# Attention stage: four of a quad's 32 row maxima are taken by ScalarE and GpSimd

## The chip, the cores and the metric

The kernel runs on one core of a Trainium2 chip. The metric is device time in microseconds (us), the median of several runs. Before the change it is 6462.87 us (three runs, 6459.95 to 6463.46). The engines are TensorE (PE in the profile; its weight loads are PEld), VectorE (DVE), ScalarE (ACT), GpSimd (POOL), and SyncE (SP), which issues the DMAs.

## The reference

Sixteen batches of 1024 tokens with 256 features go through differential attention with 16 heads (each with two score maps of head dimension 8), then through an expert layer in which each of 32 experts picks 8 tokens. Only the attention core is touched by the change:

```python
q = rope(q).transpose(0, 2, 1, 3) * scaling
k = rope(k).transpose(0, 2, 1, 3)
scores = jnp.einsum('bhqd,bhkd->bhqk', q, k)
probs = jax.nn.softmax(scores.astype(jnp.float32), axis=-1)
w = probs[:, :, 0] - lam * probs[:, :, 1]
attn = jnp.einsum('bhqk,bhkd->bhqd', w, v)
```

The softmax needs the maximum of each score row of 1024 keys before the exponentials are taken.

## The kernel before

The program has stages that follow each other: `project`, `attend`, `route`, `experts`, `scatter`. The change is in `attend` (L448), which runs from about 593 us to about 5816 us of the span. There are 512 score maps, handled in 128 *quads* of four. For each quad two things are computed:

- *Trials* (`attempt`, L769): for quad n+1, 32 tiles of 128 queries x 1024 keys. Each is two matmuls into one of two PSUM buffers `ps_m` (`j % 2`), and `maximum` (L662) on VectorE reduces it to the row maximum in `largest`. The first matmul of trial j waits (L774) until trial j-2 has been reduced.
- *Scores* (`score`, L740): for quad n, 64 transposed tiles of 128 keys x 512 queries, into one of three PSUM slots `ps_e`. ScalarE takes their exponentials (L650). The row maximum is already subtracted, since three extra rows of `q_stack` hold it, split into three bf16 parts. Score j waits (L747) for the exponential of score j-3.

`weighted_sums` (L753) multiplies the exponentials, with the values, into `ps_o`. A quad has 16 *periods* g. In each, TensorE issues in order: score 0 and half of trial 2g, score 1 and the other half, the weighted sums of two periods ago, score 2 and half of trial 2g+1, score 3 and the other half (`period`, L782). VectorE's order is `period` at L687: maximum 2g, then the transposes due in this period, then maximum 2g+1. The transposes are:

- g = 0: `turn_maxima` of the second side (c = 1, trials 16 to 31); g = 8: that of the next quad's first side (c = 0, trials 0 to 15);
- g = 1 and g = 9: `turn_sums`; g = 2: `invert`; g = 7: `turn_out`.

After `turn_maxima`, GpSimd runs `split` (L577: five small instructions), then SyncE runs `load_rows` (L522): it stores the parts to memory with four DMAs, waits until they have landed, and loads them into the extra rows of `q_stack` with one more DMA. TensorE waits for these rows (`rows_loaded`, L787) ahead of score 0 of period 0 (first side) and of period 8 (second side). GpSimd also runs `finish` (L591), which ends the quad before. SyncE's order in a quad is `turn` (L545): rows of side 0, values, rows of side 1, then `load_stacks` (18 DMAs, 1.5 MB, for the quad four ahead, once the last score of the present quad is done), then `store`.

Below, the *mark* of a period is the start of ScalarE's exponential of its score 2. In the traces a row of four exponentials begins at each mark.

Of the kernel before, what the change touches and what calls it, by code (L numbers as in the profile page):

```python
# [45 lines left out]
EPS = 1e-5  # L46
THETA = 0.0001
# [30 lines left out]
class Build:  # L78
# [369 lines left out]
    def attend(self):  # L448
# [22 lines left out]
        loops = quads // BUFS - 1  # L471
        with ExitStack() as ctx:
# [10 lines left out]
            zeros, negated, rest = sb("zeros", [P, BLK]), sb("negated", [P, BLK]), sb("rest", [P, BLK])  # L483
# [25 lines left out]
            out_stored, pool_step = [sem("out_stored0"), sem("out_stored1")], sem("pool_step")  # L509
            ONES = 5  # L510
            SPLIT_STEPS, FINISH_STEPS = 4, 10
# [3 lines left out]
            def _(sp):  # L515
# [53 lines left out]
            def _(pool):  # L569
# [7 lines left out]
                def split(h, base):  # L577

                    pool.wait_ge(max_turned, h + 1)
                    nc.gpsimd.tensor_tensor(negated[:], zeros[:], largest_t[:], ALU.subtract).then_inc(pool_step, 1)  # L580
                    if not (isinstance(h, int) and h == 0):
                        pool.wait_ge(max_stored, 16 * (P // BLK) * h)
                    nc.gpsimd.tensor_tensor(parts[:, 0], zeros[:], largest_t[:], ALU.subtract).then_inc(pool_step, 1)
                    pool.wait_ge(pool_step, base + 2)
                    nc.gpsimd.tensor_tensor(rest[:], negated[:], parts[:, 0], ALU.subtract).then_inc(pool_step, 1)
                    pool.wait_ge(pool_step, base + 3)
                    nc.gpsimd.tensor_tensor(parts[:, 1], rest[:], zeros[:], ALU.add).then_inc(pool_step, 1)
                    pool.wait_ge(pool_step, base + 4)
                    nc.gpsimd.tensor_tensor(parts[:, 2], rest[:], parts[:, 1], ALU.subtract).then_inc(split_done, 1)

# [29 lines left out]
                def turn(n, rows, base):  # L620
                    if rows:
                        for c in range(2):
                            split(2 * (n + AHEAD) + c, base)
                            base = base + SPLIT_STEPS
                    finish(n, base)

                for h in range(2 * AHEAD):
                    split(h, SPLIT_STEPS * h)
                pool.wait_ge(lam_done, 1)
                start, steps = 2 * AHEAD * SPLIT_STEPS, 2 * SPLIT_STEPS + FINISH_STEPS  # L630
                with hinted(nc, pool, 0, loops) as i:
                    for u in range(BUFS):
                        turn(BUFS * i + u, True, start + steps * (BUFS * i + u))
                for u in range(BUFS):
                    n = BUFS * loops + u
                    turn(n, u < BUFS - AHEAD, start + steps * n - 2 * SPLIT_STEPS * max(0, u - (BUFS - AHEAD)))

            @block.scalar
            def _(act):
                act.wait_ge(lam_dots, 1)  # L640
                nc.scalar.activation(lam_exp[:], lam_dot[:], ACT.Exp).then_inc(lam_exps, 1)
                act.sem_inc(exp_done, SLOTS)
                with hinted(nc, act, 0, loops + 1) as i:
                    for u in range(BUFS):
                        n = BUFS * i + u
                        for j in range(HALVES):
                            act.wait_ge(scores_done, HALVES * n + j + 1)
                            if j % QUAD == 0:
                                act.wait_ge(sums_done, GROUPS * n + j // QUAD + 1 - E_GROUPS + E_GROUPS)
                            nc.scalar.activation(e[:, j % E_BUFS], ps_e[:, (HALVES * u + j) % SLOTS], ACT.Exp,  # L650
                                                 scale=SCALE).then_inc(exp_done, 1)

            @block.vector
            def _(dve):
# [7 lines left out]
                def maximum(m, u, j):  # L662
                    dve.wait_ge(tries_done, TRIES * m + j + 1)
                    nc.vector.reduce_max(largest[:, u % 2, j // SIDE, j % SIDE:j % SIDE + 1], ps_m[:, j % 2], AX.X).then_inc(max_done, 1)  # L664

                def turn_maxima(m, u, c):

                    dve.wait_ge(max_done, TRIES * m + SIDE * (c + 1) + 2)
# [18 lines left out]
                def period(n, u, g, tries, rows=True, last_quad=True, this_quad=True):  # L687
                    if tries:
                        maximum(n + AHEAD, u + AHEAD, 2 * g)
                    if g == 0 and rows:  # L690
                        turn_maxima(n, u, 1)
                    if g == TILES and rows:
                        turn_maxima(n + 1, u + 1, 0)
# [41 lines left out]
            def _(pe):  # L735
# [33 lines left out]
                def attempt(m, u, j, half):  # L769
# [3 lines left out]
                    if half == 0:  # L773
                        pe.wait_ge(max_done, TRIES * m + j + 1)  # L774
# [777 lines left out]
```

## Time and profile before

| | before |
|---|---|
| median of three runs | 6462.87 us |
| the profiled execution | 6450.77 us (span 6449.0 us) |
| PE busy | 5794.4 us (90%) |
| DVE busy | 5879.4 us (91%) |
| ACT busy | 4718.1 us (73%) |
| POOL busy | 1947.2 us (30%) |
| granted TensorE clock, mean | 0.96; 0.99 to 1.00 in most of `attend` |
| row maxima, L664 | 4096 of 1211 ns each |
| exponentials, L650 | 8192 of 602 ns each |

The busy shares are means over the whole program. In the middle of `attend` the windows show more: between 3000 and 4000 us VectorE is busy for 978 us, TensorE for 953, ScalarE for 824 and GpSimd for 247. Instructions of one engine overlap at their ends, so that a group's time on the engine is read from the spacing of its starts and not from the mean duration. A row of the timeline merges consecutive instructions of one group; `x4` is their number, and the bracket says how long the engine stood idle ahead of the row and who ended that.

### The profile page before, as it was taken

To read this page: it belongs to the slowest core of one execution; us is meant where nothing else is said; L and a number is where in the kernel's file an instruction comes from. 1 tells how busy PE (TensorE), PEld (TensorE's weight loads), DVE (VectorE), ACT (ScalarE), POOL (GpSimd) and SP (SyncE) were. 2 spreads that over 40 slices of the span, in tenths; PEclk is the share of its full clock that TensorE was granted. 3 is DMA by queue.
4 is the path that set the end of the run, shared out by engine and by line. 5 is a ranking of instruction groups with operands and counts; after the bars stand their busy time and mean duration, and the time that the engine had idled before them with its cause. 6 is when DMAs were issued, how large, how long until landed. Compare 5 with 4: busy or idle time off the path is not lost. (4 is left out here: it accounts for less than half of the span.)

```text
span 6449.0 us, 136849 instructions
## 1 busy us (share of the span) xinstructions
PE 5794.4 (90%) x36560; PEld 1816.8 (28%) x36560; DVE 5879.4 (91%) x6456; ACT 4718.1 (73%) x8950; POOL 1947.2 (30%) x3270
## 2 busy tenths in 40 slices
PE   7776999999999999999999999999999999997775
PEld 4442222222222222222222222222222222224423
DVE  7998999999999999999999999999999999986716
ACT  4553878888788888887888888888878888783304
POOL 6774222222222222222222222222222222225506
PEclk8886999999999999999999999999999999998878
DMA  4554222222222222222222222222222222205688
GB/s 145 152 160 121 40 46 48 48 48 50 46 48 48 48 48 48 48 48 48 48 48 48 48 48 48 48 48 48 48 48 48 48 48 48 47 19 179 197 314 282
DMA packets 435720, 491.57 MB, mean 76 GB/s; under 512 B 106451, under 2 KB 288883, under 8 KB 435171
## 3 DMA queue, kind: packets, MB, share of 16 engines
q1 hardware_dynamic: 434147, 483.60, 31.2%
q8 instruction: 359, 5.88, 0.4%
q14 instruction: 190, 1.56, 0.1%
q10 hardware_dynamic: 1024, 0.53, 0.0%
HBM read 360.60 MB, written 123.21 MB: 75 GB/s over the span
## 5 line engine op out<-in xcount | busy, mean ns | idle before, releaser
L650 ACT ACTIVATE at_e<-at_ps_e 128x512 f32<-128x512 f32 x8192 | 4236.1, 602 | 944.1 <-PE at_ps_e L748 943.9
L664 DVE TENSOR_REDUCE at_largest<-at_ps_m 128x1 f32<-128x1024 f32 x4096 | 4777.2, 1211 | 156.4 <-PE at_ps_m L775 95.9
L775 PE MATMUL at_ps_m<-k_stack,q_stack 48*128 48x512 bf16 x8192 | 2725.2, 387 | 159.7 <-DVE at_largest L664 112.3
L748 PE MATMUL at_ps_e<-q_stack,k_stack 51*128 51x512 bf16 x8192 | 2478.6, 383 | 154.3 <-ACT at_e L650 69.1
L763 PE MATMUL at_ps_o<-at_e,at_v 128*32 128x512 f32 x16384 | 2255.2, 623 | 0.1
L748 PEld LDWEIGHTS at_ps_e<-q_stack,k_stack 51*128 51x128 bf16 x8192 | 624.5, 94 | 2520.6 <-ACT at_e L650 2216.6
L580 POOL TENSOR_TENSOR at_negated<-at_zeros,at_largest_t 128x32 f32<-128x32 f32 x256 | 64.8, 253 | 3244.3 <-DVE at_largest_t L671 3244.3
L775 PEld LDWEIGHTS at_ps_m<-k_stack,q_stack 48*128 48x128 bf16 x8192 | 620.1, 93 | 924.0 <-DVE at_largest L664 884.9
L763 PEld LDWEIGHTS at_ps_o<-at_e,at_v 128*32 128x32 f32 x16384 | 450.3, 149 | 525.5 <-issue 340.3
L615 POOL TENSOR_TENSOR at_rms<-at_mean_eps,at_minus_half 128x16 f32<-128x16 f32 x128 | 372.7, 2912 | 10.0
L429 PE MATMUL pr_ps_q<-pr_xn_t,pr_w 128*128 128x512 f32 x512 | 232.8, 597 | 1.5 <-issue 0.8
L676 DVE STREAM_TRANSPOSE at_sums_t<-at_ps_o 128x512 f32<-128x512 f32 x256 | 180.3, 704 | 28.8 <-PE at_ps_o L763 28.6
L312 ACT CAST pr_parts<-pr_rotated 128x1024 bf16<-128x1024 f32 x64 | 66.7, 1043 | 177.4 <-DVE pr_rotated L373 177.4
L271 POOL TENSOR_TENSOR pr_swapped<-pr_swapped,pr_sin 128x1024 f32<-128x1024 f32 x64 | 164.5, 2571 | 97.7 <-DVE pr_swapped L387 97.7
L595 POOL TENSOR_TENSOR at_inverse<-at_inverse,at_neg_lam 128x16 f32<-128x16 f32 x128 | 27.8, 217 | 539.5 <-DVE at_inverse L680 539.5
L263 POOL TENSOR_TENSOR pr_parts<-pr_rest,pr_parts 128x1024 bf16<-128x1024 f32 x64 | 182.4, 2851 | 11.8 <-ACT pr_parts L316 11.8
L1016 ACT ACTIVATE ro_x<-ro_ps_y,ro_y_bias,ro_y_rstd 128x256 f32<-128x256 f32 x128 | 61.9, 564 | 163.7 <-POOL ro_y_bias L978 163.7
L417 PE MATMUL pr_ps_t<-ident,pr_xn 128*128 128x128 f32 x256 | 59.6, 410 | 125.6 <-ACT pr_xn L298 72.7
L609 POOL TENSOR_TENSOR at_square<-at_square 128x128 f32<-128x128 f32 (+3 forms) x512 | 158.5, 309 | 40.1
L379 DVE TENSOR_TENSOR pr_rest<-pr_rotated,pr_parts 128x1024 f32<-128x1024 f32 x64 | 168.6, 2635 | 0.0
L439 PE MATMUL pr_ps_v<-pr_w,pr_xn_t 128*128 128x256 f32 x512 | 159.4, 468 | 2.4 <-ACT pr_v_out L331 2.4
L373 DVE TENSOR_TENSOR pr_rotated<-pr_by_cos,pr_swapped 128x1024 f32<-128x1024 f32 x64 | 143.1, 2236 | 9.3 <-issue 9.3
(128 smaller groups left out, 3082.2 us busy)
## 6 DMA issues: line engine op xcount, KB each, us to landing
k_stack<-k_parts SPq DMA_DIRECT2D x1536, 64.0 KB
q_stack<-q_parts SPq DMA_DIRECT2D x256, 192.0 KB
q_stack<-q_parts SPq DMA_DIRECT2D x256, 128.0 KB
w_first<-in_w SPq DMA_DIRECT2D x32, 1024.0 KB, 11.7
ex_w_second<-in_w SPq DMA_DIRECT2D x32, 1024.0 KB, 12.7
q_parts<-pr_parts SPq DMA_DIRECT2D x96, 256.0 KB, 2.9
k_parts<-pr_parts SPq DMA_DIRECT2D x96, 256.0 KB, 2.9
pr_x_in<-in_x SPq DMA_DIRECT2D x16, 1024.0 KB, 6.2
```

What stands on the lines that cost most here:

```text
L263: nc.gpsimd.tensor_tensor(parts[:, ch, 2], rest[:, ch % 2], parts[:, ch, 1], ALU.subtract).then_inc(part3_done, 1)
L271: nc.gpsimd.tensor_tensor(swapped[:, ch % 2], swapped[:, ch % 2], sin[:], ALU.mult).then_inc(sin_done, 1)
L379: nc.vector.tensor_tensor(rest[:, ch % 2], rotated[:, ch % 2], parts[:, ch, 0], ALU.subtract).then_inc(rest_done, 1)
L429: last = nc.tensor.matmul(ps_q[:, ch % 2, half * HALF:(half + 1) * HALF], w[:, k, ch // KC, cols], xn_t[:, u, k, half * HALF:(half + 1) * ...
L439: last = nc.tensor.matmul(ps_v[:, ch % 2, j * D:(j + 1) * D], xn_t[:, u, k, t * P:(t + 1) * P], w[:, k, 2, :], start=(k == 0), stop=(k == ...
L615: nc.gpsimd.tensor_tensor(rms[:], mean_eps[:], minus_half[:], ALU.pow).then_inc(pool_step, 1)
L650: nc.scalar.activation(e[:, j % E_BUFS], ps_e[:, (HALVES * u + j) % SLOTS], ACT.Exp, scale=SCALE).then_inc(exp_done, 1)
L664: nc.vector.reduce_max(largest[:, u % 2, j // SIDE, j % SIDE:j % SIDE + 1], ps_m[:, j % 2], AX.X).then_inc(max_done, 1)
L676: nc.vector.transpose(sums_t[:, c].rearrange("p b d -> p (b d)"), ps_o[:]).then_inc(sums_read, 1)
L748: nc.tensor.matmul(ps_e[:, (HALVES * u + j) % SLOTS], k_stack[rows, u, pair, c, kt * P:(kt + 1) * P], q_stack[rows, u, pair, c, half * HAL ...
L763: last = nc.tensor.matmul(ps_o[32 * tile:32 * tile + 32, :], v[:, u, tile // 2, kt::TILES], e[:, (QUAD * g + tile) % E_BUFS], start=(kt == ...
L775: last = nc.tensor.matmul(ps_m[:, j % 2, half * HALF:(half + 1) * HALF], q_stack[rows, u, pair, c, t * P:(t + 1) * P], k_stack[rows, u, pa ...
```

## The change

- VectorE no longer reduces trials 5, 15, 19 and 25 of a quad (`FOLDED`), each the second trial of its period: of the periods 2, 7, 9 and 12. ScalarE copies such a trial (128x1024) from PSUM to `fold_in` after the fourth exponential of that period. GpSimd folds the copy twice (1024 to 512 to 256). A fold is a maximum built of three instructions: subtract, clamp at zero, add. VectorE then reduces two folded trials in one instruction (2 x 256), inside `turn_maxima`.
- `turn_maxima` moves from periods 0 and 8 to periods 2 (side 1) and 12 (side 0). It now waits for the folds.
- The maxima are reduced with a sign change, and `split` loses one of its five instructions.
- GpSimd's order per quad becomes: split of side 1, finish, folds 0 and 1, split of side 0, folds 2 and 3.
- SyncE issues `load_stacks` ahead of the rows of side 1.
- TensorE's trial two behind a folded one waits for ScalarE's copy.

```diff
+        FOLDED = (5, 15, 19, 25)
+        REDUCED = TRIES - FOLDS
+        TURNS = (TILES + 4, 2)
...
                     if rows:
                         load_rows(n + AHEAD, (u + AHEAD) % BUFS, 0)
                         load_v(n + AHEAD, (u + AHEAD) % BUFS)
-                        load_rows(n + AHEAD, (u + AHEAD) % BUFS, 1)
                     if load:
                         sp.wait_ge(scores_done, HALVES * (n + 1))
                         load_stacks(n + BUFS, u)
+                    if rows:
+                        load_rows(n + AHEAD, (u + AHEAD) % BUFS, 1)
                     store(n, u)
...
+                def fold(m, k, base):
+                    c, x = k // 2, fold_in[:, k % 2]
+                    pool.wait_ge(copied, FOLDS * m + k + 1)
+                    for width in (S // 2, S // 4):
+                        low, high = x[:, 0:width], x[:, width:2 * width]
+                        nc.gpsimd.tensor_tensor(high, high, low, ALU.subtract).then_inc(pool_step, 1)
+                        pool.wait_ge(pool_step, base + 1)
+                        pool.sem_inc(passed, 1)
+                        nc.gpsimd.tensor_scalar(high, high, LARGEST, 0.0, ALU.min, ALU.max).then_inc(pool_step, 1)
+                        pool.wait_ge(pool_step, base + 2)
+                        if width > WIDTH:
+                            nc.gpsimd.tensor_tensor(low, low, high, ALU.add).then_inc(pool_step, 1)
+                            pool.wait_ge(pool_step, base + 3)
+                            base = base + 3
+                        else:
+                            if not (isinstance(m, int) and m == 0):
+                                pool.wait_ge(folds_read, 2 * m + c - 1)
+                            nc.gpsimd.tensor_tensor(fold_out[:, c, k % 2], low, high, ALU.add).then_inc(fold_done, 1)
...
+                def turn(n, this, following, base):
+                    if this:
+                        split(2 * n + 1, base)
+                        base = base + SPLIT_STEPS
+                    finish(n - 1, base)
+                    base = base + FINISH_STEPS
+                    if following:
+                        base = folds(n + AHEAD, (0, 1), base)
+                        split(2 * (n + AHEAD), base)
+                        folds(n + AHEAD, (2, 3), base + SPLIT_STEPS)
...
+                def copy_trial(m, k):
+                    act.wait_ge(tries_done, TRIES * m + FOLDED[k] + 1)
+                    if not (isinstance(m, int) and m == 0 and k < 2):
+                        act.wait_ge(fold_done, FOLDS * m + k - 1)
+                    nc.scalar.copy(fold_in[:, k % 2], ps_m[:, FOLDED[k] % 2]).then_inc(copied, 1)
...
+                        if tries and j % QUAD == QUAD - 1 and j // 2 in FOLDED:
+                            copy_trial(n + AHEAD, FOLDED.index(j // 2))
...
                 def turn_maxima(m, u, c):
-                    dve.wait_ge(max_done, TRIES * m + SIDE * (c + 1) + 2)
+                    dve.wait_ge(fold_done, FOLDS * m + 2 * (c + 1))
+                    first, second = FOLDED[2 * c] % SIDE, FOLDED[2 * c + 1] % SIDE
+                    columns = slice(first, second + 1, second - first)
+                    nc.vector.tensor_reduce(largest[:, u % 2, c, columns], fold_out[:, c], AX.X, ALU.max,
+                                            negate=True).then_inc(folds_read, 1)
+                    dve.wait_ge(folds_read, 2 * m + c + 1)
+                    dve.wait_ge(max_done, REDUCED * m + REDUCED // 2 * (c + 1) + 2)
...
-                    if half == 0:
-                        pe.wait_ge(max_done, TRIES * m + j + 1)
+                    if half == 0 and j - 2 in FOLDED:
+                        pe.wait_ge(copied, FOLDS * m + FOLDED.index(j - 2) + 1)
+                    elif half == 0:
+                        pe.wait_ge(max_done, REDUCED * m + (reduced_before(j - 1) if j else -1) + 2)
```

## Rows read from the trace of the kernel before

**Rows 1.** The page's group of the exponentials, line 650.

```profile
L650 ACT ACTIVATE at_e<-at_ps_e 128x512 f32<-128x512 f32 x8192 | 4236.1, 602 | 944.1 <-PE at_ps_e L748 943.9
```

**Rows 2.** The tile at_e: duration min/median/max in ns, first and last start.

```profile
L650 ACT ACTIVATE at_e<-at_ps_e x8192: 590/598/653, 634.3 to 5813.3; 128x512 f32<-128x512 f32 x200
```

**Rows 3.** Timeline (start us, us), ACT, periods 2 to 4, 8 to 11 of one quad.

```profile
3112.62 2.07 ACT L650 ACTIVATE at_e<-at_ps_e 128x512 f32<-128x512 f32 x4 [0.36 <-PE at_ps_e L748]
3115.28 2.06 ACT L650 ACTIVATE at_e<-at_ps_e 128x512 f32<-128x512 f32 x4 [0.59 <-PE at_ps_e L748]
3117.74 2.06 ACT L650 ACTIVATE at_e<-at_ps_e 128x512 f32<-128x512 f32 x4 [0.40 <-PE at_ps_e L748]
...
3127.43 2.06 ACT L650 ACTIVATE at_e<-at_ps_e 128x512 f32<-128x512 f32 x4 [0.36 <-PE at_ps_e L748]
3130.09 2.07 ACT L650 ACTIVATE at_e<-at_ps_e 128x512 f32<-128x512 f32 x4 [0.59 <-PE at_ps_e L748]
3132.53 2.07 ACT L650 ACTIVATE at_e<-at_ps_e 128x512 f32<-128x512 f32 x4 [0.37 <-PE at_ps_e L748]
3135.30 2.06 ACT L650 ACTIVATE at_e<-at_ps_e 128x512 f32<-128x512 f32 x4 [0.71 <-PE at_ps_e L748]
```

**Rows 4.** Timeline, ACT, periods 10 and 11 of the quad before that.

```profile
3092.98 2.06 ACT L650 ACTIVATE at_e<-at_ps_e 128x512 f32<-128x512 f32 x4 [0.36 <-PE at_ps_e L748]
3095.64 2.06 ACT L650 ACTIVATE at_e<-at_ps_e 128x512 f32<-128x512 f32 x4 [0.60 <-PE at_ps_e L748]
```

**Rows 5.** Timeline, PE, one regular period from score 0 to the next score 2.

```profile
3061.79 0.38 PE L748 MATMUL at_ps_e<-q_stack,k_stack 51*128 51x512 bf16 x1
...
3062.42 0.39 PE L748 MATMUL at_ps_e<-q_stack,k_stack 51*128 51x512 bf16 x1
...
3062.74 1.09 PE L763 MATMUL at_ps_o<-at_e,at_v 128*32 128x512 f32 x8
3063.77 0.39 PE L748 MATMUL at_ps_e<-q_stack,k_stack 51*128 51x512 bf16 x1
```

**Rows 6.** Timeline, DVE: ten maxima back to back, then a transpose.

```profile
3073.06 11.78 DVE L664 TENSOR_REDUCE at_largest<-at_ps_m 128x1 f32<-128x1024 f32 x10
3084.76 0.70 DVE L685 STREAM_TRANSPOSE at_out<-at_attn_t 128x512 f32<-128x512 f32 x1
```

**Rows 7.** Groups by line and shape, ACT: instructions on 1024 elements.

```profile
L1262 ACT ACTIVATE ex_hidden<-ex_ps_h 128x1024 f32<-128x1024 f32 x8 | 8.2, 1024 | 65.3 <-PE ex_ps_h L1305 65.3
L316 ACT CAST pr_parts<-pr_rest 128x1024 bf16<-128x1024 f32 x64 | 66.9, 1045 | 82.1 <-DVE pr_rest L379 80.5
```

**Rows 8.** Groups by line and shape, POOL.

```profile
L271 POOL TENSOR_TENSOR pr_swapped<-pr_swapped,pr_sin 128x1024 f32<-128x1024 f32 x64 | 164.5, 2571 | 97.7 <-DVE pr_swapped L387 97.7
L598 POOL TENSOR_TENSOR at_normed<-at_sums_t,at_inverse 128x512 f32<-128x512 f32 x128 | 135.5, 1058 | 10.0
L604 POOL TENSOR_TENSOR at_square<-at_attn 128x256 f32<-128x256 f32 x128 | 78.6, 614 | 10.0
L580 POOL TENSOR_TENSOR at_negated<-at_zeros,at_largest_t 128x32 f32<-128x32 f32 x256 | 64.8, 253 | 3244.3 <-DVE at_largest_t L671 3244.3
L1249 POOL COPY ex_tokens<-merged_t 128x256 f32 x8 | 3.2, 400 | 150.4 <-PE ex_ps_o L1322 117.1 <-PEq L1286 33.3
```

**Rows 9.** Timeline, SP: stacks issued first, then rows of side 0, then of side 1.

```profile
3114.08 1.16 SPq L59 DMA_DIRECT2D q_stack<-q_parts  x3
...
3129.86 1.83 SPq L528 DMA_DIRECT2D max_parts<-at_parts  x4
3135.66 0.78 SPq L531 DMA_DIRECT2D q_stack<-max_parts  x1
...
3149.41 1.83 SPq L528 DMA_DIRECT2D max_parts<-at_parts  x4
3152.26 0.78 SPq L531 DMA_DIRECT2D q_stack<-max_parts  x1
```

**Rows 10.** DMA issues by line: count, KB each, median us to landing.

```profile
at_v<-v_tiles SPq DMA_DIRECT2D x128, 128.0 KB, 2.2
```

More of the change, by code:

```diff
@@ L46 @@
 EPS = 1e-5
+LARGEST = float(np.finfo(np.float32).max)
 THETA = 0.0001
@@ L471, in attend, with reduced_before @@
         loops = quads // BUFS - 1
+        FOLDED = (5, 15, 19, 25)
+        FOLDS = len(FOLDED)
+        WIDTH = S // 4
+        REDUCED = TRIES - FOLDS
+        TURNS = (TILES + 4, 2)
+        def reduced_before(j):
+            return sum(i not in FOLDED for i in range(j))
         with ExitStack() as ctx:
@@ L618, in finish, with folds @@
                                             ALU.mult).then_inc(attn_done, 1)
[L620 to L628, printed above, removed]
+                def folds(m, ks, base):
+                    for k in ks:
+                        fold(m, k, base)
+                        base = base + FOLD_STEPS
+                    return base
@@ L629, in _ @@
+                for c in range(2):
+                    base = folds(0, (2 * c, 2 * c + 1), base)
+                    split(c, base)
+                    base += SPLIT_STEPS
+                base = folds(1, (0, 1), base)
+                split(2, base)
+                base = folds(1, (2, 3), base + SPLIT_STEPS)
                 pool.wait_ge(lam_done, 1)
-                start, steps = 2 * AHEAD * SPLIT_STEPS, 2 * SPLIT_STEPS + FINISH_STEPS
+                steps = 2 * SPLIT_STEPS + FINISH_STEPS + FOLDS * FOLD_STEPS
@@ L631, in _ @@
                 with hinted(nc, pool, 0, loops) as i:
                     for u in range(BUFS):
[L633 to L636, printed above, removed]
+                        turn(BUFS * i + u + 1, True, True, base + steps * (BUFS * i + u))
+                base += steps * BUFS * loops
@@ new lines, in turn @@
+                def turn(n, u, tries):
+                    for j in range(HALVES):
+                        act.wait_ge(scores_done, HALVES * n + j + 1)
+                        if j % QUAD == 0:
+                            act.wait_ge(sums_done, GROUPS * n + j // QUAD + 1 - E_GROUPS + E_GROUPS)
+                        nc.scalar.activation(e[:, j % E_BUFS], ps_e[:, (HALVES * u + j) % SLOTS], ACT.Exp,
+                                             scale=SCALE).then_inc(exp_done, 1)
+                        if tries and j % QUAD == QUAD - 1 and j // 2 in FOLDED:
+                            copy_trial(n + AHEAD, FOLDED.index(j // 2))
@@ L640, in _ @@
+                for k in range(FOLDS):
+                    copy_trial(0, k)
                 act.wait_ge(lam_dots, 1)
                 nc.scalar.activation(lam_exp[:], lam_dot[:], ACT.Exp).then_inc(lam_exps, 1)
-                act.sem_inc(exp_done, SLOTS)
-                with hinted(nc, act, 0, loops + 1) as i:
+                with hinted(nc, act, 0, loops) as i:
                     for u in range(BUFS):
[L645 to L651, printed above, removed]
+                        turn(BUFS * i + u, u, True)
@@ L653, in _ @@
+                for u in range(BUFS):
+                    turn(BUFS * loops + u, u, u < BUFS - AHEAD)
             @block.vector
@@ L689, in period @@
                         maximum(n + AHEAD, u + AHEAD, 2 * g)
-                    if g == 0 and rows:
+                    if g == TURNS[1] and rows:
                         turn_maxima(n, u, 1)
-                    if g == TILES and rows:
+                    if g == TURNS[0] and tries:
                         turn_maxima(n + 1, u + 1, 0)
```

27 lines of the change are left out of this document (18 added, 9 removed).

## The prediction, made before the changed kernel was run

> **What bounds the kernel now.** I read the page first. It shows VectorE and TensorE about equally busy over the program, so the shares do not say which of them sets the pace. I then read the attention stage period by period. The 8192 exponentials run from 634.3 to 5813.3 us [rows 2], which is 5179.0/128 = 40.46 us a quad. The timeline of ScalarE gives the length of each period as the distance of two marks. A regular period takes 2.42 us, and sixteen of these are 38.8. In the quad of [rows 3] five periods are longer: 2 to 3 takes 2.66, 3 to 4 takes 2.46, 8 to 9 2.66, 9 to 10 2.44 and 10 to 11 2.77, together 0.89 us above 5 x 2.42. The quads that follow the loop's back edge, one in four, have 0.24 there in their second half in place of 0.61 [rows 4]. The mean extra is 0.80 us a quad. The rest of the 40.46, some 0.9, is waiting at the loop edges, which the change leaves alone.
>
> What sets the 2.42? TensorE's rows show it [rows 5]: score 1 (3062.42) waits for the exponential that began at the mark 3061.77, since that frees its slot (0.65 after the mark). The weighted sums follow at +0.32, the next score 2 at +1.03 more (3063.77), and its exponential starts 0.42 later, the next mark. 0.65 + 0.32 + 1.03 + 0.42 = 2.42. This is a ring of TensorE and ScalarE, with no VectorE in it. VectorE needs 11.70/10 = 1.17 us per maximum [rows 6], so 2.34 in a regular period, and 0.63 more where it transposes 512 columns. It falls behind in the periods with transposes and regains 0.08 a period. What it is late by shows up as the 0.80. So **VectorE costs the ring 0.80 us a quad, and nothing can be gained from relieving it beyond that**, although it is busy nearly all the time.
>
> How much room has ScalarE in the ring? Four exponentials span 2.06 with a last duration of 0.60 [rows 1, 3], so they start 0.487 apart. Four take 1.95, and 0.47 of the period's 2.42 is free.
>
> **The change part by part.** All sums are for 127 quads, those in which trials run beside scores, against the profiled execution of 6450.8 us. The median of the runs shown is 12.1 above it.
>
> *Removed: the lateness of VectorE.* Four of 32 maxima go, 4 x 1.17 = 4.7 us a quad. Two reductions of 2 x 256 elements come back; by the transpose of 512 columns they take 0.63 each. In periods 2, 7, 9 and 12 VectorE now has 1.17 + at most 1.1 us, within 2.42. Period 1 keeps two maxima and a transpose, 0.55 us over, but before the change it was followed by a delay only when period 0's and 2's small work was added. I take the whole 0.80 as gone: -0.80 x 127 = **-102 us**; bounds -102 and -60 (period 1 keeps a third).
>
> *Added: the copy on ScalarE.* Before is no copy of 1024 elements out of PSUM. The nearest row is the activation of 1024 from PSUM, 1024 ns; a cast of 1024 in SBUF has 1045 [rows 7]. Instructions of ScalarE overlap by 0.602 - 0.487 = 0.115, so the copy takes 0.91 to 0.93 of the engine; I take 0.92. It stands behind the exponential of score 3, with those of the next scores 0 and 1 and then score 2, the next mark, behind it. That mark comes at 4 x 0.487 + 0.92 = 2.87 after its own, not 2.42. The 0.47 free in the period is used up and 0.44 to 0.45 is left over. It is not regained: the following score 1 waits for the delayed exponential, and the ring starts anew from there with its 2.42. So 4 x 0.44 x 127 = **+224 us**. Bounds: 0.42 if the overlap is as large as seen (213), 0.57 if the copy has no overlap at either end (290).
>
> The Trainium skill gives another price for this copy (ScalarE: Activation LUTs, What ACT_TABLE_LOAD costs): 186 ns plus 0.833 ns an element, with an overlap of 93 between neighbours. It would be 0.946 us here and 237 us in place of 224; the exponentials' 602 stand beside its 612. The same page prices a change of the table set at 2.7 us, which would be ruinous with copies among exponentials; in this trace copies and exponentials share the routing stage without such a load.
>
> *Added: folds on GpSimd.* Four instructions with two inputs and two with one, per trial. At 512 elements a two-input instruction takes 1.06, half of the 1024-element row's 2.57 would be 1.29; at 256 it takes 0.61 [rows 8]. For the clamp the lower bound is the copy, 0.40 at 256 and some 0.63 at 512; for the upper bound I take twice a two-input instruction. With 0.08 between dependent ones a trial takes 4.8 to 7.9 us; I take 5.4 (clamp near the copy's row, since it has one input). Cover: side 1 is the tighter. Its two folds run after the split of side 0 (about 2.3 after the mark of period 12) and must end at VectorE's turn in period 2 of the next quad, 13.7 us later. So 6.8 us a trial is free, and at 5.4 this costs **0**. ScalarE's copy also waits for the fold two before; that is done 2.9 us ahead.
>
> The Trainium skill advises elementwise work on VectorE, since GpSimd is about half as fast with two inputs (GPSIMD Engine Reference, 4.1 Engine selection). Its 2.6 cycles an element at 1.2 GHz are 1.11 us for 512; the row's 1.06 agrees. By it the move costs GpSimd some 22 us a quad, which the idle engine has.
>
> *Moved: the turn of side 0, from period 8 to 12.* From turn to landed rows it takes: split 4 x 0.33 (0.25 each, [rows 8], and a gap), issue and landing of the parts 2.85, from 3149.41 to 3152.26 [rows 9], then 2.2 as for the values [rows 10], some 6.6 in all. The turn ends its reduce near 0.95 behind the mark, so the rows land at +7.6. TensorE needs them ahead of score 0 of the next quad, which is issued at the mark of period 15: 3 x 2.42 + 0.44 = +7.7, and may slip by 0.4 more before score 1 is late. Half a microsecond of cover; single quads will miss it: **+5 us**, bounds 0 and +40.
>
> *Moved: SyncE's 18 stack loads ahead of the rows of side 1.* Here the trace has a warning. In the quad of [rows 9] the parts of side 0 were issued at 3129.86, 15.8 us after the stacks (3114.08), and the next step came only 5.80 us later, not 2.85: parts queue behind stacks still under way, until some 20 us after their first issue. In other quads the stacks are through after 13 to 17. Now the parts of side 1 always queue behind them. The stacks start 2.4 us ahead of the quad's first mark, so the rows land 13 to 21 us after it; they are needed by 7 x 2.42 + 0.44 + 0.4 = 17.8. A quarter of the quads is late by a microsecond or so: **+38 us**, bounds 0 and +115.
>
> *Start and end.* Before the first quad VectorE waits for the folds of trials 15 and 25, less the four maxima: **+3 us**. The final quad is as before.
>
> Sum: -102 + 224 + 0 + 5 + 38 + 3 = +168. 6450.8 + 168 = 6619, and 12 for the median: **6630 us**.
>
> **Rivals.** *The copies are covered (faster).* If the copy's 0.92 found room in the ring, as it would if the three `ps_e` slots let ScalarE work ahead, only the -102 would be left: 6361 us. For it speaks that ScalarE is busy for 73% only. Against it: its idle time comes in pieces of 0.36 to 0.47 once a period [rows 3], and the slots are refilled only as fast as it empties them. It decides if the exponential behind the copy starts the next mark before 2.42 + 0.20, for then 4 x 0.20 equals the 0.80. Chance 0.09.
>
> *A draw.* Half of a copy's excess is hidden and the rows come in time: 6440 to 6475 us. Chance 0.03.
>
> *The folds become the bound (slower still).* From 6.8 us a trial on, each 0.1 more costs 0.2 us a quad, because VectorE stands in `turn_maxima` with all later maxima behind it, and TensorE behind those. At 7.6 it is 1.6 x 127 = 203, so 6833 us. The clamp is the one instruction with no row. Chance 0.08.
>
> *The rows of side 1 are late in most quads.* Stacks and parts then take 20 us each time, as in [rows 9]: 3 us a quad for most, some 250 us, 6840 us. Chance 0.04.
>
> The forecast itself (the copies exposed, the folds hidden) has 0.76; its own range is 6560 to 6720.
>
> **How the numbers follow.** Low end: copies 213, lateness -102, no late rows, and 60 us less waiting at loop edges if the stack loads' new place frees the instruction fetches: 6514; I take 6530. High end: copies 290, lateness -60, rows 40 and 115: 6849 for all at once; I take 6750, which leaves out most of the two slow rivals. A measurement of this kernel can tell 0.2%, 13 us, from no change. Faster 0.09, same 0.03, slower 0.88.
>
> **What would show it.** Right: ScalarE's marks 2.42 apart except after periods 2, 7, 9 and 12, with 2.85 to 2.9 there; no idle of ScalarE in these four; the longer periods of [rows 3] gone; VectorE idle some 4 us a quad more; the copy near 1.02 us; a fold's six instructions within 6.8 us. Late rows would show as a wait of TensorE ahead of score 0 of period 8. Wrong: periods with a copy at 2.42 (first rival), or VectorE idle ahead of the 2 x 256 reduction (third).

## The result and the profile after

The changed kernel takes 6669.86 us (median of four runs, 6632.57 to 6688.60) against 6461.99 us before: a ratio of 1.0315, with a 95% interval from 1.0270 to 1.0359. It is slower by 208 us. The profiled execution took 6688.60 us against 6450.77, 238 us more; the sums below are made against that. Two later comparisons of the same kernel gave 1.0441 and 1.0408 (6744.66 and 6713.44 us). What varied is told with the experiments.

The page of the changed kernel, with busy time and share:

```profile
span 6686.8 us, 145310 instructions
PE 5835.6 (87%) x36560; PEld 1835.6 (27%) x36560; DVE 5534.0 (83%) x6200; ACT 5146.6 (77%) x9462; POOL 4426.4 (66%) x6086
L704 ACT ACTIVATE at_e<-at_ps_e 128x512 f32<-128x512 f32 x8192 | 4258.2, 618 | 751.6 <-PE at_ps_e L822 750.2
L697 ACT COPY at_fold_in<-at_ps_m 128x1024 f32<-128x1024 f32 x512 | 522.4, 1020 | 43.1 <-PE at_ps_m L851 43.1
```

VectorE really has been relieved: 5534 us where it had 5879, and between 3000 and 4000 us of the span 864 us where it had 978. The program is longer all the same. The tile at_e gives the length of the attention stage, as [rows 2] did (durations in ns, then first and last start):

```profile
L704 ACT ACTIVATE at_e<-at_ps_e x8192: 588/606/686, 638.4 to 6050.2; 128x512 f32<-128x512 f32 x200
```

5411.8/128 = 42.28 us a quad where [rows 2] gave 40.46. That is 1.82 more, and the stage starts 4 us later; together this is all of the 238.

Where in the quad? ScalarE's timeline answers to [rows 3] (start, duration, idle before). The first exponential of a period is its mark. The rows show periods 2 to 7, then 9:

```profile
3273.62 1.08 ACT L704 ACTIVATE at_e<-at_ps_e 128x512 f32<-128x512 f32 x2 [0.36 <-PE at_ps_e L822]
3274.59 1.02 ACT L697 COPY at_fold_in<-at_ps_m 128x1024 f32<-128x1024 f32 x1
3275.48 3.08 ACT L704 ACTIVATE at_e<-at_ps_e 128x512 f32<-128x512 f32 x6
3278.92 2.06 ACT L704 ACTIVATE at_e<-at_ps_e 128x512 f32<-128x512 f32 x4 [0.36 <-PE at_ps_e L822]
3281.35 2.06 ACT L704 ACTIVATE at_e<-at_ps_e 128x512 f32<-128x512 f32 x4 [0.36 <-PE at_ps_e L822]
...
3286.20 1.08 ACT L704 ACTIVATE at_e<-at_ps_e 128x512 f32<-128x512 f32 x2 [0.36 <-PE at_ps_e L822]
...
3291.49 1.09 ACT L704 ACTIVATE at_e<-at_ps_e 128x512 f32<-128x512 f32 x2 [0.36 <-PE at_ps_e L822]
3292.47 1.02 ACT L697 COPY at_fold_in<-at_ps_m 128x1024 f32<-128x1024 f32 x1
3293.36 3.08 ACT L704 ACTIVATE at_e<-at_ps_e 128x512 f32<-128x512 f32 x6
3296.80 2.06 ACT L704 ACTIVATE at_e<-at_ps_e 128x512 f32<-128x512 f32 x4 [0.36 <-PE at_ps_e L822]
```

Two exponentials, the copy, then six exponentials without a gap: ScalarE has nothing free there. From the mark of period 2 (3273.62) to that of period 4 (3278.92) it is 5.30 us, where two regular periods take 4.85. One copy costs the ring 0.45 to 0.46 us. Periods 9 and 10 show the same, 3291.49 to 3296.80.

The mean length of each period in us, worked out from the starts of the exponentials of 122 quads (the third to the 124th):

```
period          0    1    2    3   4-6    7    8    9   10   11   12   13   14   15   quad
before        2.42 2.42 2.66 2.46 2.42 3.12 2.62 2.44 2.75 2.42 2.42 2.42 2.42 2.63  40.50
after         2.46 2.42 2.83 2.47 2.42 3.91 2.57 2.83 2.47 2.42 2.83 2.47 2.42 2.96  42.34
b_relief      2.43 2.42 2.66 2.42 2.42 3.24 2.49 2.42 2.42 2.42 2.42 2.42 2.42 2.63  40.11
a_nofold      2.44 2.43 2.83 2.47 2.42 3.69 2.58 2.83 2.47 2.43 2.83 2.47 2.43 2.95  42.12
a_copy2       2.43 2.42 3.73 2.48 2.42 3.93 2.66 3.73 2.60 2.47 3.74 2.59 2.49 2.63  45.17
a_sp          2.45 2.43 2.83 2.47 2.42 3.55 2.53 2.83 2.47 2.43 2.83 2.47 2.42 2.95  41.92
a_sp_turn11   2.42 2.42 2.83 2.47 2.42 3.63 2.53 2.83 2.48 2.43 2.94 2.43 2.42 2.63  41.74
half          2.42 2.45 2.45 2.42 2.42 2.78 2.66 2.43 2.45 2.42 2.45 2.42 2.42 2.63  39.69
b_sp          2.42 2.42 2.66 2.46 2.42 4.57 2.66 2.44 2.65 2.42 2.42 2.42 2.42 2.63  41.90
after_again   2.44 2.42 2.83 2.47 2.42 4.38 2.66 2.83 2.47 2.42 2.83 2.47 2.42 2.86  42.79
after_third   2.43 2.43 2.83 2.47 2.42 4.20 2.60 2.83 2.47 2.43 2.83 2.47 2.43 2.80  42.48
a_sp_again    2.44 2.43 2.83 2.47 2.42 3.52 2.54 2.83 2.49 2.43 2.83 2.47 2.43 2.88  41.87
```

The names are those of the experiments. Period 7 holds the wait at the loop's back edge in one quad of four, and period 15 a fixed 0.80 in another, before the change too.

Besides the copies two more places grew. In period 7 TensorE waits for the rows of side 1, which it needs ahead of score 0 of period 8. SyncE's timeline of a quad in which this happened (its first mark is at 3433.15, and it does not follow the back edge):

```profile
3431.11 1.13 SPq L60 DMA_DIRECT2D q_stack<-q_parts  x3
...
3435.93 2.13 SPq L66 DMA_DIRECT2D k_stack<-k_parts  x6
3441.17 1.87 SPq L541 DMA_DIRECT2D max_parts<-at_parts  x4
3451.06 0.78 SPq L544 DMA_DIRECT2D q_stack<-max_parts  x1
```

ScalarE's in its period 7:

```profile
3450.57 1.09 ACT L704 ACTIVATE at_e<-at_ps_e 128x512 f32<-128x512 f32 x2 [0.36 <-PE at_ps_e L822]
3451.54 1.02 ACT L697 COPY at_fold_in<-at_ps_m 128x1024 f32<-128x1024 f32 x1
3454.01 1.08 ACT L704 ACTIVATE at_e<-at_ps_e 128x512 f32<-128x512 f32 x2 [1.45 <-PE at_ps_e L822]
3456.51 2.06 ACT L704 ACTIVATE at_e<-at_ps_e 128x512 f32<-128x512 f32 x4 [1.42 <-PE at_ps_e L822]
```

and TensorE's, with score 0 of period 8 first:

```profile
3453.51 0.38 PE L822 MATMUL at_ps_e<-q_stack,k_stack 51*128 51x512 bf16 x1 [2.75 <-DMA q_stack<-max_parts]
...
3454.15 1.79 PE L837 MATMUL at_ps_o<-at_e,at_v 128*32 128x512 f32 x8
3455.87 0.61 PE L822 MATMUL at_ps_e<-q_stack,k_stack 51*128 51x512 bf16 x1
```

The parts were issued 10.1 us behind the first stack load, and the step after them came 9.89 us later and not 2.85 as in [rows 9] without stacks under way. The load of the rows (3451.06) then landed at 3453.39, and TensorE went on. The period took 5.94 us, 3.11 more than a copy explains. A part of that is TensorE itself, which ran at the lower of its two clock levels for a while behind the wait: the weighted sums took 1.79 us where [rows 5] has 1.09, and the granted clock was 0.65 in the mean between 3453.5 and 3456.5 us.

Over the 122 quads of the trace: the step from the issue of the parts of side 1 to the load of the rows took 6.5 us in the mean (2.9 to 11.1), where it was 3.0 before. The load itself took 2.3 to 2.5 us from issue to landing, every time and in both kernels. In 40 quads the rows landed after TensorE could have used them. None of the 40 is a quad behind the back edge: there the rows had landed by the mark of period 7 each time, so the wait at the back edge is for something else.

The view of waits puts 132.6 us of TensorE's idle time, in 115 waits, on the loads of the rows of both sides. About two thirds stand in period 7 (0.73 us a quad). The rest (0.33 a quad) stands in period 15, where TensorE waits for the rows of side 0, whose turn has moved to period 12.

### The profile page after: what moved, and what is told of

It reads as the page before. It is cut to its first block and busy times, and to the rows that moved or that the text cites. A ratio compares the mean times of both kernels' runs of the same rounds, so it can differ in the third digit from the quotient of the medians.

```text
span 6686.8 us, 145310 instructions
## 1 busy us (share of the span) xinstructions
PE 5835.6 (87%) x36560; PEld 1835.6 (27%) x36560; DVE 5534.0 (83%) x6200; ACT 5146.6 (77%) x9462; POOL 4426.4 (66%) x6086
## 3 DMA queue, kind: packets, MB, share of 16 engines
q14 instruction: 219, 1.79, 0.1%
q10 hardware_dynamic: 1024, 0.53, 0.0%
## 5 line engine op out<-in xcount | busy, mean ns | idle before, releaser
L731 DVE TENSOR_REDUCE at_largest<-at_ps_m 128x1 f32<-128x1024 f32 x3584 | 4237.5, 1217 | 679.8 <-PE at_ps_m L851 644.3
L822 PE MATMUL at_ps_e<-q_stack,k_stack 51*128 51x512 bf16 x8192 | 2648.0, 388 | 428.7 <-DMA q_stack<-max_parts 132.6
L851 PE MATMUL at_ps_m<-k_stack,q_stack 48*128 48x512 bf16 x8192 | 2812.3, 391 | 80.1 <-DVE at_largest L731 44.7
L837 PE MATMUL at_ps_o<-at_e,at_v 128*32 128x512 f32 x16384 | 2285.1, 630 | 0.1
L610 POOL TENSOR_TENSOR at_fold_in<-at_fold_in 128x512 f32<-128x512 f32 (+1 forms) x1024 | 1023.9, 1000 | 74.9 <-ACT at_fold_in L697 34.2
L596 POOL TENSOR_TENSOR at_parts<-at_largest_t,at_zeros 128x32 bf16<-128x32 f32 x256 | 64.3, 251 | 1147.4 <-DVE at_largest_t L745 1147.4
L616 POOL TENSOR_TENSOR at_fold_in<-at_fold_in 128x512 f32<-128x512 f32 x512 | 650.1, 1270 | 42.9
L613 POOL TENSOR_SCALAR at_fold_in<-at_fold_in 128x512 f32<-128x512 f32 (+1 forms) x1024 | 518.2, 506 | 202.8 <-POOL at_fold_in L610 199.9
L697 ACT COPY at_fold_in<-at_ps_m 128x1024 f32<-128x1024 f32 x512 | 522.4, 1020 | 43.1 <-PE at_ps_m L851 43.1
L622 POOL TENSOR_TENSOR at_fold_out<-at_fold_in 128x256 f32<-128x256 f32 x512 | 371.9, 726 | 53.5 <-POOL at_fold_in L613 21.1
```

The costliest lines, as they stand in the source:

```text
L610: nc.gpsimd.tensor_tensor(high, high, low, ALU.subtract).then_inc(pool_step, 1)
L613: nc.gpsimd.tensor_scalar(high, high, LARGEST, 0.0, ALU.min, ALU.max).then_inc(pool_step, 1)
L616: nc.gpsimd.tensor_tensor(low, low, high, ALU.add).then_inc(pool_step, 1)
L622: nc.gpsimd.tensor_tensor(fold_out[:, c, k % 2], low, high, ALU.add).then_inc(fold_done, 1)
L697: nc.scalar.copy(fold_in[:, k % 2], ps_m[:, FOLDED[k] % 2]).then_inc(copied, 1)
L731: nc.vector.tensor_reduce(largest[:, u % 2, j // SIDE, j % SIDE:j % SIDE + 1], ps_m[:, j % 2], AX.X, ALU.max, negate=True).then_inc(max_do ...
```

## The experiments

Times are medians beside the kernel before on the same chip; each such comparison gives a ratio.

**b_relief: the relief alone.** The kernel before, less four maxima:

```diff
+        LEFT_OUT = (5, 15, 19, 25)
                 def maximum(m, u, j):
+                    if j in LEFT_OUT:
+                        return
                     dve.wait_ge(tries_done, TRIES * m + j + 1)
```

> The kernel before, with the row maxima of trials 5, 15, 19 and 25 of each quad left out altogether (nobody reads these four trials) and nothing put in their place. It prices the relief of VectorE by itself. Theory (the ring of TensorE and ScalarE sets the period, VectorE's lateness costs 0.80 us a quad): 102 us less than before, 6360 us, and every period at 2.42 us. Rival (the busiest engine is the bound): 4 x 1.17 us a quad less, 594 us, 5870 us. Second rival (the five long periods have another cause than VectorE): no change, 6462 us.

Measured: 6403.67 us against 6453.13, ratio 0.9927 (0.9906 to 0.9947). So 49 us less, not 594: VectorE's busy share was no bound. The long periods 8, 9 and 10 are at 2.42 in three quads of four. The extra 0.24 in period 2 stays, as ScalarE's timeline shows:

```profile
3125.71 2.07 ACT L656 ACTIVATE at_e<-at_ps_e 128x512 f32<-128x512 f32 x4 [0.36 <-PE at_ps_e L756]
3128.37 2.06 ACT L656 ACTIVATE at_e<-at_ps_e 128x512 f32<-128x512 f32 x4 [0.59 <-PE at_ps_e L756]
3130.80 2.06 ACT L656 ACTIVATE at_e<-at_ps_e 128x512 f32<-128x512 f32 x4 [0.36 <-PE at_ps_e L756]
```

Period 1 still has two maxima and a transpose there. So of the 0.80 us a quad 0.56 went (71 us). Periods 7 and 8 of the quads behind the back edge took 8.44 us together, 7.79 before, which takes 0.16 a quad (20 us) back. The size expected for this run was too large, the mechanism was right.

**a_nofold: the folds made cheap.** Of each fold's three instructions only the last add stays.

> The changed kernel with the folds cut to their last add each (subtract and clamp are left out of both folds, so that the folded maxima are not maxima). GpSimd's work per trial falls from 5.65 us to about 2. Theory (the folds are hidden): within 20 us of the changed kernel, 6650 to 6690 us. Rival (the folds hold up VectorE's turn or slow its neighbours): 50 us less or more, 6620 us or below.

Measured: 6652.40 us, ratio 1.0323 (1.0288 to 1.0358), where the changed kernel had 1.0315. All periods but 7 and, slightly, 8, 0 and 15 are as in the changed kernel. Period 7 is 0.22 shorter; the total alone could not tell this from the changed kernel's own spread (6670 to 6745 us). VectorE's reduction of the folded trials settles it. In the changed kernel it waited for a fold only before the first quad:

```profile
L739 DVE TENSOR_REDUCE at_largest<-at_fold_out 128x2 f32<-128x512 f32 x256 | 172.4, 674 | 9.7 <-POOL at_fold_out L622 9.7
```

In the 122 quads the last fold had ended at least 1.75 us ahead of it. The folds cost nothing. GpSimd's groups in the changed kernel show what they take of GpSimd:

```profile
L610 POOL TENSOR_TENSOR at_fold_in<-at_fold_in 128x512 f32<-128x512 f32 x512 | 651.0, 1271 | 34.2 <-ACT at_fold_in L697 34.2
L613 POOL TENSOR_SCALAR at_fold_in<-at_fold_in 128x512 f32<-128x512 f32 x512 | 313.6, 613 | 102.9 <-POOL at_fold_in L610 100.0 <-issue 2.9
L610 POOL TENSOR_TENSOR at_fold_in<-at_fold_in 128x256 f32<-128x256 f32 x512 | 373.0, 728 | 40.7 <-POOL at_fold_in L616 0.7
L613 POOL TENSOR_SCALAR at_fold_in<-at_fold_in 128x256 f32<-128x256 f32 x512 | 204.6, 400 | 99.9 <-POOL at_fold_in L610 99.9
```

Two instructions of 1271, one of 613, two of 728 and one of 400 make 5.01 us; with the gaps a trial takes 5.65, inside the 6.8 that were free.

**a_copy2: the copy twice.**

```diff
+                    nc.scalar.copy(spare[:, k % 2], ps_m[:, FOLDED[k] % 2])
                     nc.scalar.copy(fold_in[:, k % 2], ps_m[:, FOLDED[k] % 2]).then_inc(copied, 1)
```

> The changed kernel with each trial copied twice by ScalarE, the first time into a tile that nobody reads. Theory (behind the first copy ScalarE has no room left in the ring): each further copy costs its full 0.91 us, 4 x 0.91 x 127 = 462 us more than the changed kernel's 6670, so 7130 us, unless part of it hides behind the wait for the rows of side 1 in period 7 (then 115 less, 7015). Rival (ScalarE, busy for 77%, takes copies in its idle time): less than 200 more, below 6870 us.

Measured: 7061.88 us, ratio 1.0952 (1.0928 to 1.0977): 392 more than the changed kernel's median, between the two numbers given. The timeline of ScalarE in period 2:

```profile
3399.02 1.08 ACT L706 ACTIVATE at_e<-at_ps_e 128x512 f32<-128x512 f32 x2 [0.36 <-PE at_ps_e L824]
3399.99 1.02 ACT L698 COPY at_spare<-at_ps_m 128x1024 f32<-128x1024 f32 x1
3400.89 1.04 ACT L699 COPY at_fold_in<-at_ps_m 128x1024 f32<-128x1024 f32 x1
3401.79 3.09 ACT L706 ACTIVATE at_e<-at_ps_e 128x512 f32<-128x512 f32 x6
3405.23 1.08 ACT L706 ACTIVATE at_e<-at_ps_e 128x512 f32<-128x512 f32 x2 [0.35 <-PE at_ps_e L824]
```

The copies start 0.90 apart, and periods 2, 9 and 12 are 3.73 where they were 2.83: every further copy costs its full 0.90. Periods 10 and 13, behind such copies, are 0.13 and 0.12 longer as well. In 17 and 18 of the 122 quads TensorE had the lower clock level there; period 10 took 3.31 us in these and 2.48 in the others. In period 7 the second copy was almost free (3.93 against 3.91), since the wait for the rows stood there anyway, and the wait in period 15 went, which fits the 0.9 us more that the rows of side 0 have from period 12 on.

**a_sp: SyncE's old order in the changed kernel.** The rows of side 1 are again issued ahead of the stack loads.

> The changed kernel with SyncE's old order: rows of side 1 first, the 18 stack loads behind them. Theory (in periods 7 to 8 the changed kernel waits for rows that queue behind the stacks, some 0.8 us a quad): 100 us less than the changed kernel, 6570 us, period 7 to 8 at 2.83 us except at the loop's back edge. Rival (that wait belongs to the later turn and split, or the queue is slow in any order): within 20 us of 6670.

Measured: 6630.02 us, ratio 1.0273 (1.0251 to 1.0296). Period 7 is 2.83 except at the back edge, as expected, and the total is 60 us above the number given. The gain beside the changed kernel's first measurement is only 40 us, because the waits at the back edge grew again: periods 7 and 8 of these quads took 8.45 us together, 6.87 in the changed kernel, 7.79 before. In the changed kernel the largest of 30 such pairs was 8.1 us; with the old order 8 of 30 took 10.8 to 13.7 (before the change 7 of 30 took 10.7 to 15.2).

**b_sp: that order in the kernel before.** One edit: stack loads ahead of the rows of side 1.

> The kernel before with one edit: SyncE issues the 18 stack loads ahead of the rows of side 1. Theory (the rows of side 1 then queue behind the stacks and reach period 8 late, whatever the turn; and the long waits at the loop's back edge are code that waits behind the same stacks and goes when these come earlier): period 7 to 8 longer by 0.8 to 1.5 us in three of four quads, no wait over 4 us at the back edge where the kernel before has 8 in 30; together 50 us more than before, 6500 us. Rival (the rows are late in the changed kernel because their turn moved from period 0 to 2): no change, 6450 us, period 7 to 8 at 2.42.

Measured: 6636.43 us against 6459.11, ratio 1.0290 (1.0262 to 1.0319). This was the surprise. The reordering of SyncE's DMAs alone costs 177 us, three and a half times what I had expected. SyncE's timeline:

```profile
3191.98 2.13 SPq L65 DMA_DIRECT2D k_stack<-k_parts  x6
3194.41 2.00 SPq L528 DMA_DIRECT2D max_parts<-at_parts  x4
3206.83 0.81 SPq L531 DMA_DIRECT2D q_stack<-max_parts  x1
```

and ScalarE's in period 7:

```profile
3206.46 1.09 ACT L651 ACTIVATE at_e<-at_ps_e 128x512 f32<-128x512 f32 x2 [0.36 <-PE at_ps_e L749]
3210.05 1.08 ACT L651 ACTIVATE at_e<-at_ps_e 128x512 f32<-128x512 f32 x2 [2.50 <-PE at_ps_e L749]
```

The four small DMAs of 3 KB, issued right behind the last stack load, held SyncE for 12.4 us until they had landed; over 122 quads this step took 10.2 us in the mean (4.4 to 14.1). The load behind it landed 2.4 us after its issue, as everywhere. ScalarE stood idle for 2.50 us. The turn is in period 0 here, so the rival is refuted: neither the later turn nor the split makes the rows late. And with the stacks first no pair of periods 7 and 8 at the back edge took more than 7.7 us, as in the changed kernel.

Why so much more than 50? In the quads that do not follow the back edge the rows came 181 us too late in sum, but periods 7 and 8 grew by 234. The difference is TensorE's clock, as the stretches around the wait in this quad show (length, busy time of PE, PEld, DVE, ACT and POOL, then granted clock, DMA share and GB/s):

```profile
3206.40:3209.40 3.00, 0.32 (x5) 0.08 (x1) 1.97 (x3) 1.09 (x2) 0.00 (x0) 0.90 0.10 25
3209.40:3212.40 3.00, 3.00 (x14) 0.59 (x16) 1.34 (x2) 1.08 (x2) 0.46 (x2) 0.50 0.13 31
```

TensorE was busy for 0.32 of 3.00 us, and then worked at a granted clock of 0.50, the 1.2 GHz level, with a score's matmul at 0.60 us and not 0.38. In 50 of the 63 quads with late rows the clock fell in this way, in none of the 29 others. The earlier stack loads gave some 53 us back at the back edge (periods 7 and 8 there: 6.03, before 7.79). I had priced neither the length of the wait nor the clock behind it.

**after_again, after_third, a_sp_again.** The changed kernel twice more, and beside the second of these a_sp once more; no edits.

> The changed kernel once more, unaltered, on the chip of the other run. Theory: 200 us more than before, 6655 us, the same long periods (2, 7, 9, 12 and 15), no wait over 4 us at the back edge. Rival (the absence of long waits at the back edge was chance): some are back, and 30 us more.

> The changed kernel, unaltered, beside the next one on the same chip, since its time differed by 75 us between two chips (6670 and 6745) while the kernel before moved by 10. Theory (what differs is how long the stack transfers take, and with it the wait in period 7 to 8): any time from 6640 to 6750, with the difference in period 7 to 8 alone.

> The changed kernel with SyncE's old order, on the same chip as the unaltered one. Theory (the old order takes away the wait for the rows of side 1 and gives back the long waits at the back edge): 6620 to 6640 us on any chip, 40 to 115 us less than the unaltered one here. Rival (the difference between the chips has another cause than the queue behind the stacks): it moves with the unaltered kernel, and the two differ by 40 us at most whatever that takes.

Measured: after_again 6744.66 us, ratio 1.0441 (1.0424 to 1.0459); after_third 6713.44 us, 1.0408 (1.0382 to 1.0434), and beside it on the same chip a_sp_again 6633.62 us, 1.0278 (1.0255 to 1.0300). The kernel before stayed at 6459. The 6745 is 90 us above the 6655 expected; after_third and a_sp_again lie within what was given. The table shows what differed between the first and the second measurement of the changed kernel: period 7 (3.91 and 4.38), a little of period 8, and nothing else that grew. It goes with the step behind the parts of side 1. That took 6.5, 7.0 and 7.5 us in the mean where period 7 took 3.91, 4.20 and 4.38, and 6.1 in a_nofold with its 3.69. With the old order the time was the same both times, 6630 and 6634. So the order costs the changed kernel 80 us (6713 - 6634) where both ran side by side on one chip, and its size varies from one comparison to the next. What makes the stacks slower in one run than in another, the chip or something else, stays open. The first measurement was the mildest of the three. The expected absence of long waits at the back edge held in all three (the largest pairs were 8.1, 8.3 and 8.2 us). That they are fetches of code which queue behind the stacks fits this, but was not shown: *half*, below, has the old order and fewer long waits (8 of 30 pairs took 8.9 us or more, the other 22 only 5.1).

**a_sp_turn11: the turn of side 0 a period earlier.** SyncE has the old order here too.

```diff
-        TURNS = (TILES + 4, 2)
+        TURNS = (TILES + 3, 2)
```

> The changed kernel with SyncE's old order and the turn of side 0 in period 11 in place of 12. Theory (the wait of 0.2 to 0.9 us ahead of the quad's first score, in three of four quads, is for the rows of side 0, which the turn in period 12 starts too late): it goes, 0.33 x 127 = 42 us less than with the old order alone (6630), so 6590 us, and period 15 to 16 is 2.42 us save at one quad in four. Rival (that wait has another cause, such as values or code that arrive then): within 15 us of 6630.

Measured: 6621.37 us, ratio 1.0269 (1.0252 to 1.0286). The wait in period 15 is gone (2.63 in the mean, all of it the fixed 0.80 of one quad in four, as before the change). So it was the wait for the rows of side 0. The total fell by 9 us only: period 12 grew by 0.11, and periods 7 and 8 at the back edge by 0.36. The total agrees with the rival's number as well and does not settle the 42 us; the period does.

This run has neither wait for late rows, so that beside b_relief it has the copies, the folds and the moved turns: 41.74 and 40.11 us a quad. The difference of 1.63 is near 1.60, four copies at 0.46 less the 0.24 of period 2 that the copy there covers.

**half: a version that beats both.** Trials 1, 3, 19 and 23 are shared: VectorE reduces the first 512 columns, ScalarE copies the other 512. GpSimd folds them to 128, which VectorE reduces together with its own partial maximum. Turns in periods 11 and 0; SyncE in the old order.

```diff
+        FOLDED = (1, 3, 19, 23)
+        WIDTH = S // 8
+        TURNS = (TILES + 3, 0)
...
+                    nc.scalar.copy(fold_in[:, k % 2], ps_m[:, FOLDED[k] % 2, HALF:]).then_inc(copied, 1)
...
+                        nc.vector.reduce_max(fold_out[:, k // 2, k % 2, WIDTH:], ps_m[:, j % 2, 0:HALF], AX.X).then_inc(max_done, 1)
...
+                    elif j - 2 in FOLDED:
+                        pe.wait_ge(copied, FOLDS * m + FOLDED.index(j - 2) + 1)
```

> A version meant to beat both. Four trials (1, 3, 19, 23) are shared: VectorE reduces their first 512 columns, ScalarE copies only the second 512 (0.48 to 0.50 us of the engine, against 0.47 free in a period's ring), GpSimd folds these to 128, and VectorE takes the folded rest with its own partial maximum in one reduction per side. The turns come in periods 11 and 0 and SyncE has the old order. Theory (only what exceeds ScalarE's 0.47 us of room costs anything): periods with a copy take 2.42 to 2.47 us, the long periods 8 to 11 of the kernel before go, the 0.24 in period 2 to 3 stays as it did without four maxima; some 50 us less than before, 6400 us. Rival (each copy delays the ring by a fixed cost, by its waits or by what it displaces, whatever its size): 2.6 us or more in each of the four periods, 6480 us or more.

Measured: 6364.42 us against 6450.59, ratio 0.9872 (0.9856 to 0.9889), 86 us less than before, where 50 was expected. ScalarE in periods 0 to 2, both copies of side 0 among them:

```profile
3092.71 1.09 ACT L704 ACTIVATE at_e<-at_ps_e 128x512 f32<-128x512 f32 x2 [0.36 <-PE at_ps_e L826]
3093.68 0.59 ACT L697 COPY at_fold_in<-at_ps_m 128x512 f32<-128x512 f32 x1
3094.15 2.10 ACT L704 ACTIVATE at_e<-at_ps_e 128x512 f32<-128x512 f32 x4
3096.11 0.62 ACT L697 COPY at_fold_in<-at_ps_m 128x512 f32<-128x512 f32 x1
3096.57 3.10 ACT L704 ACTIVATE at_e<-at_ps_e 128x512 f32<-128x512 f32 x6
3100.03 2.06 ACT L704 ACTIVATE at_e<-at_ps_e 128x512 f32<-128x512 f32 x4 [0.36 <-PE at_ps_e L826]
```

Two copies of half the size in neighbouring periods, and from 3092.71 to 3100.03 there are 7.32 us for three periods, 0.05 above the 7.27 of three regular ones. A half copy occupies ScalarE for 0.47 (3093.68 to 3094.15) and costs 0.02 to 0.03; a whole one 0.89 to 0.90 and costs 0.46. The room of 0.47 is where the price begins. One expectation missed: the 0.24 of period 2 is gone, which fits that period 1 has half a maximum less, and 0.24 stays in period 8 behind the transpose of period 7. Not all of the 86 us is the relief's. In the table the quad is 0.81 shorter; 0.30 of it (38 us) is the back edge, where periods 7 and 8 took 6.58 us together and 7.79 before. Why that wait shrank is not shown, and the waits there differ between runs (8.44 in b_relief). The rest, 0.51 a quad or 65 us, stands in periods that have nothing to do with it.

## Why the prediction was right, and where its sum was off

The forecast was 6630 us from a sum of +168; the first measurement was 6670 and the profiled execution +238, inside the range of 6530 to 6750. The later 6713 and 6745 are inside it too, the last one just, and outside the 6560 to 6720 that I had given the forecast itself. Term by term, against the profiled execution:

| term | forecast | measured | from |
|---|---|---|---|
| VectorE's lateness | -102 | -103 | extras of periods 2, 3, 8, 9, 10 gone or covered: 0.81 x 127 |
| four copies a quad | +224 | +234 | 4 x 0.46 x 127 |
| folds | 0 | 0 | VectorE never waits for one; a_nofold |
| rows of side 0, turn in period 12 | +5 | +47 | periods 15 and 0: 0.37 x 127 |
| rows of side 1 behind the stacks, less the back edge | +38 | +58 | periods 7 and 8: 0.79 lost, 0.34 regained, x 127 |
| start | +3 | +4 | first exponential 638.4, was 634.3 |

The terms sum to 240; the rest of 2 is rounding.

**The ring.** Read from one period of TensorE and ScalarE, it held in every kernel: 2.42 us wherever nothing was added, whether VectorE had 32 or 28 whole maxima a quad. Half, whole and double copies (0.47, 0.90 and 1.79 us of ScalarE) cost 0.03, 0.46 and 1.37 us: the excess over 0.47, as forecast, and 0.03 to 0.05 more.

**The lateness.** The sum was right for the changed kernel and its reason was half right. Alone, the relief brings 0.56 and not 0.80 (b_relief); this is the bound "period 1 keeps a third", which I had named and not taken. In the changed kernel the remaining 0.24 falls into period 2, which has a copy, and is covered by it: the period is 2.83 as every other with a copy, while TensorE's wait for VectorE's maxima is still there (0.27 us a quad in period 2; 0.28 before and in b_relief).

**The copy.** 1020 ns against 1024 from the activation's row, 0.89 to 0.90 of the engine against 0.92. The ring's cost came out at 0.46 and not 0.44: 0.41 in the period and 0.05 in the next. The Trainium skill's formula for an activation (ScalarE: Activation LUTs, What ACT_TABLE_LOAD costs) gives, as an estimate, 1039 ns and with its overlap of 93 an occupation of 0.946 us; the trace has 1020 ns and 0.90 us, and the trace's number is the one used here.

**The rows of side 0** are the term that was mis-sized by most, ninefold. The chain was read 0.3 us too short: the rows landed 7.9 to 8.0 us behind the mark of period 12 in the median, not 7.6, where TensorE needs them at 7.7. So they are a little late in every quad, which costs 0.16 and 0.22 us in two quads of four. The rest is a tail. In one quad of four the rows are late by 1.8 to 3.6 us in 11 of 30 turns of the loop, 0.97 us in the mean, and period 0 behind such a wait is longer at the lower clock level. I had priced a thin cover by the typical quad, where the mean is made by the tail.

**The rows of side 1.** The step was named with its evidence, the 5.80 us in [rows 9], and where the rows would land was right: 13.6 to 21.4 us after the first mark, forecast 13 to 21. How often they come too late was near the quarter forecast as well: periods 7 and 8 grew in 37 of 122 quads. The size of one lateness was wrong, 2.6 us in the mean and not "a microsecond or so". That is 0.79 a quad, or 100 us, in place of 38. The relief at the back edge, counted only for the low end of the range, gives 44 of it back (6.87 - 0.46 = 6.41 us for periods 7 and 8 there, 7.79 before). That this gain, which the sum leaves out, hid most of the error is luck. Nor has the sum a term for the clock: in the changed kernel's profiled execution it is small (the rows came 92 us too late in sum, periods 7 and 8 grew by 97), in b_sp it is a quarter of what these periods grew by. b_sp also shows that this edit alone, in the kernel before, costs more (177) than the copies less their relief do (234 - 103 = 131). The second rival for the slow side, "late in most quads", which had a chance of 0.04, was not so in the first measurement (40 of 122). In the second it was, if barely (68 of 122), with 170 us lost and not 250.

**The rivals.** Covered copies and a draw are refuted by a_copy2 and by the 2.83. Folds as the bound: refuted by the 5.65 us a trial and by VectorE, which never waits for one.

## What to carry to other kernels

An engine that is busy for 96% of a stage (VectorE, 4976 of 5163 us) need not set its pace. Find the ring of waits that gives a regular period, count what each engine has free in it, and size what is moved by that room: half a copy was free where a whole one cost more than the relief was worth. And when a small transfer with a deadline is put behind a large one in the same queue, the leg that is issued while the large one is under way waits for it (the second leg, issued after, did not); the price is the large one's tail, not its median. A wait that idles TensorE can cost more than its length, since the clock may be at the lower level behind it.

## What had not been expected of the hardware

- Four DMAs of 3 KB issued behind 18 stack loads of 1.5 MB in all took 12.4 us to land, and 10.2 in the mean, where alone the step takes 2.85.
- With identical code this wait differed between comparisons: period 7 was 3.91, 4.38 and 4.20 us in the mean, while the medians of the kernel before lay within 0.2%. With the rows ahead of the stacks the time was the same twice, to 4 us.
- Behind a wait of some 3 us TensorE's granted clock was 0.50 for a while. In the middle of `attend` (122 quads) this happened 10 times before the change, 68 us in all, 47 times in the changed kernel (167 us) and 54 times in b_sp (249 us).
- A GpSimd subtraction of two 512-element operands, in place, took 1271 ns, where the multiplication of [rows 8], which reads one of its inputs with a broadcast, has 1058. The clamp with one input took 613.
